# Two-layer causal attention on one Trainium2 core: the next unit's mask put between two divisions, query norms put ahead of the next input, first and last slots laid out anew

## What is computed

```python
x = x + L0(x)          # x: (64, 128, 512) float32
x = x + L1(x)

def L0(x):
    xn = layernorm(x) * g_in
    q  = (xn @ Wq) * 64 ** -0.5          # 16 heads of 64
    k, v = split(xn @ Wkv)               # one key/value head, shared by all
    k, v = null row put in front of each
    sim = q k^T + bias                   # bias: (16, 128, 128), and a null column
    sim = -max above the diagonal and at masked keys
    return layernorm(softmax(sim) v @ Wo) * g_out

def L1(x):                               # as L0, but
    q = q / |q| * q_scale                # each head's query to unit length
    k = k / |k| * k_scale
    bias = a small network of the distance between positions
```

## Time and profile before

| what | value |
|---|---|
| median of 3 runs | 2713.48 us (2711.86 to 2715.43) |
| the profiled execution: its own time | 2714.91 us |
| its span, first to last instruction | 2713.1 us |
| mean granted TensorE clock | 0.984 |
| PE busy | 2523.7 us, 93% |
| VectorE busy | 1849.5 us, 68% |
| ScalarE busy | 1696.9 us, 63% |
| GpSimd busy | 1023.0 us, 38% |
| queries of the late slot awaited by PE, in all | 90.5 us, 64 times |

### The profile page before, as it was taken

The page is one execution under the profiler, slowest core; times in us unless marked ns, Lnnn a source line. Parts: engine busy times, 40 slices in busy tenths (PEclk is TensorE's granted clock), DMA queues, the critical chain, the costliest instruction groups (busy, mean ns, idle before and its releaser), DMA issues.

```text
span 2713.1 us, 47936 instructions
## 1 busy us (share of the span) xinstructions
PE 2523.7 (93%) x13985; PEld 2093.7 (77%) x13985; DVE 1849.5 (68%) x4665; ACT 1696.9 (63%) x6621; POOL 1023.0 (38%) x1688
## 2 busy tenths in 40 slices
PE   2699999999999999999999999999999999999997
PEld 1577877877878888888788788787787787787884
DVE  5467677667667667667667667767767766766764
ACT  2366666666666666666666666666666666666663
POOL 1343343333433433433433334334334333343331
PEclk7799999999999999999999999999999999999998
DMA  6000010010010010000011011001001001001000
GB/s 204 17 30 28 22 33 29 21 33 29 21 33 29 21 33 29 21 33 29 21 33 33 21 29 33 25 25 33 29 21 33 29 21 33 29 21 33 29 17 20
DMA packets 79317, 85.10 MB, mean 31 GB/s; under 512 B 38944, under 2 KB 42048, under 8 KB 79296
## 3 DMA queue, kind: packets, MB, share of 16 engines
q1 hardware_dynamic: 74864, 82.72, 10.0%
q10 hardware_dynamic: 4432, 2.14, 0.4%
HBM read 49.15 MB, written 16.79 MB: 24 GB/s over the span
## 4 chain that ended last, share of the span: by engine, by line
PE 70%; DVE 14%; ACT 10%; issue 3%; DVEq 0%; POOL 0%
PE psum L368 22%; PE psum L300 15%; PE psum L330 13%; PE psum L354 9%; ACT probs L449 7%; PE psum L317 5%; PE psum L339 3%; DVE q_sb L529 3%; DVE xn L490 2%; DVE norm_sq L515 2%; PE psum L287 2%; DVE bn_in L483 2%; DVE probs L546 1%; DVE neg_max L552 1%; DVE k_dup L527 1%
## 5 line engine op out<-in xcount | busy, mean ns | idle before, releaser
L633 POOL TENSOR_TENSOR weights<-probs,den_inv 128x256 f32<-128x256 f32 (+1 forms) x1024 | 492.6, 507 | 1598.8 <-DVE den_inv L558 1598.8
L449 ACT ACTIVATE probs<-probs,neg_max 128x129 f32<-128x129 f32 (+1 forms) x2048 | 744.1, 366 | 507.4 <-DVE neg_max L552 507.4
L622 POOL TENSOR_TENSOR masked_bias<-bias,pad_neg 128x516 f32<-128x516 f32 (+1 forms) x512 | 477.8, 965 | 15.3 <-POOL pad_neg L616 9.2
L546 DVE TENSOR_TENSOR probs<-psum,masked_bias 128x388 f32<-128x388 f32 x512 | 287.3, 562 | 266.7 <-PE psum L330 247.1
L330 PEld LDWEIGHTS psum<-keys,q_t 128*128 128x128 f32 x2048 | 297.4, 188 | 130.7 <-issue 101.9
L330 PE MATMUL psum<-keys,q_t 128*128 128x130 f32 (+1 forms) x2048 | 392.3, 333 | 2.0 <-DVE keys L538 1.1
L449 ACT ACTIVATION_READ_ACCUMULATOR probs<-probs,neg_max 128x1 f32 x2048 | 387.1, 189 | 0.0
L300 PE MATMUL psum<-w_hi,x_hi 128*128 128x384 f32 x1536 | 348.2, 349 | 3.6 <-DVE x_lo L495 3.6
L300 PE MATMUL psum<-w_hi,x_lo 128*128 128x384 f32 x1536 | 329.7, 337 | 0.0
L300 PE MATMUL psum<-w_lo,x_hi 128*128 128x384 f32 x1536 | 329.5, 337 | 0.0
L368 PE MATMUL psum<-wo_hi,o_hi 128*128 128x512 f32 x1024 | 287.5, 423 | 2.3 <-ACT o_hi L460 2.3
(11 more groups left out here) (108 smaller groups left out, 3306.7 us busy)
## 6 DMA issues: line engine op xcount, KB each, us to landing
xa<-in_x_dram SPq DMA_DIRECT2D x64, 256.0 KB, 2.9
x_res<-in_x_dram SPq DMA_DIRECT2D x64, 256.0 KB, 2.6
x_res<-x SPq DMA_DIRECT2D x64, 256.0 KB, 2.3
out_dram<-x_out SPq DMA_DIRECT2D x64, 256.0 KB, 2.1
raw<-in_L_cond_Wq_dram SPq DMA_DIRECT2D x8, 512.0 KB, 7.6
raw<-in_L_cond_Wo_dram SPq DMA_DIRECT2D x8, 256.0 KB, 3.4
raw<-in_L_cond_Wout_dram SPq DMA_DIRECT2D x8, 256.0 KB, 3.7
v_pair<-v_diff SPq DMA_DIRECT2D x128, 16.0 KB, 1.7
```

What stands on the lines that cost most here:

```text
L449: x_ = nc.scalar.activation(s, s, ACT.Exp, bias=neg_max[:, g, b, e:e + 1], accum_out=den[:, g, b, e:e + 1])
L546: nc.vector.tensor_tensor(probs[:, g, :], SP[g % 2][:, 0:ROW], masked_bias[u.layer][:, g, :], ALU.add).then_inc(biased[g], 1)
L622: m = nc.gpsimd.tensor_tensor(block(masked_bias[u.layer][:, gs, :], b), block(bias[u.layer][:, gs, :], b), pad_neg[u.layer][:, 0:WIDTH[b]] ...
L633: m = nc.gpsimd.tensor_tensor(w, block(probs[:, g, :], b)[:, :, 1:1 + n], den_inv[:, g, b, :].unsqueeze(2).to_broadcast([P, 2, n]), ALU.mult)
```

## The change

It has four parts.

1. `body` is split into `early` and `late` slots, and `run_units` takes these and a third form, `meet`. Within the loop TensorE's order and the order of all engines in the early slot stay as they were, but for GpSimd.
2. GpSimd, in every slot: divisions of groups 0 and 1 of u, mask of w, divisions of groups 2 and 3 of u.
3. Late slot, VectorE: `norms` of banks 0 and 1 and both `unit_q` follow one another; `input_statistics` of the next input comes behind them, `normalise` behind `take_kt`. ScalarE: `square` of bank 1 stands ahead of `inverse_root` of bank 0, and `rstd_of_input` behind the copies of the transposed weights.
4. The first and last slots: A(1) is projected beside the attention of A(0), and the first and last B meet the A before them in a `meet` slot, where v's output product is finished early and B's input is made in the same slot. Ahead of the loop stand five slots (A(0) alone, then the attentions of A(0), A(1), B(0), A(2)), behind it five. The two buffers `v_diff` and `v_pair` go by the unit's number (`side`) in place of its layer, and SP's residual load of A is issued a unit ahead.

```diff
-def run_units(eng, body, nb):
+def run_units(eng, begin, early, late, meet, nb):
     A = lambda a: static_unit(0, a, nb)
     B = lambda b: static_unit(1, b, nb)
-    body(None, None, A(0), None, None)
-    body(A(0), None, A(1), None, None)
-    body(A(1), A(0), A(2), None, B(0))
-    body(A(2), A(1), A(3), B(0), B(1))
+    begin(A(0))
+    early(None, None, A(0), A(1))
+    early(A(0), None, A(1), None)
+    meet(A(1), A(0), B(0), A(2))
+    early(B(0), A(1), A(2), B(1))
+    late(A(2), B(0), B(1), A(3))
     with eng.Fori(3, nb - 1) as i:
...
-        body(a, a_prev, a_next, b_old, b_new)
-    body(A(nb - 1), A(nb - 2), None, B(nb - 3), B(nb - 2))
-    body(None, A(nb - 1), None, B(nb - 2), B(nb - 1))
-    body(None, None, None, B(nb - 1), None)
+        early(b_old, a_prev, a, b_new)
+        late(a, b_old, b_new, a_next)
+    early(B(nb - 3), A(nb - 2), A(nb - 1), B(nb - 2))
+    late(A(nb - 1), B(nb - 3), B(nb - 2), None)
+    meet(B(nb - 2), A(nb - 1), B(nb - 1), None)
+    late(B(nb - 1), B(nb - 2), None, None)
+    late(None, B(nb - 1), None, None)
```

SyncE, TensorE's `meet`, ScalarE, VectorE and GpSimd:

```diff
+            def load_next(u):
+                if u.layer == 0 and not last(u):
+                    wait_apart(sp, xn_done, u.done, sp_passed)
+                    load_xa(u.batch + 1)
+                if not last(u):
+                    wait_apart(sp, pad_neg_done, u.done, sp_passed)
+                    load_keep(u.layer, u.batch + 1)
...
+            def slot(u, v, w, n):
+                run_stages((load_next, w), (copy_v, w), (finish, v))
...
+            def meet(u, v, w, n):
+                run_stages((part(scores, (0, 1)), u), (part(project_out, 0), v), (part(project_out, 1), v),
+                           (part(project_out, 2), v), (part(scores, (2, 3)), u), (transpose_x, w),
+                           (part(project, (2, 0, 1)), w), (part(transpose_p, (0, 1, 2, 3)), u))
+                closing(u, w)
...
+            def unit_queries(u, w):
+                run_stages((part(inverse_root, 2), w), (part(square, 0), w), (part(square, 1), w), (part(inverse_root, 0), w),
+                           (part(take_pt, (0, 1)), u), (part(inverse_root, 1), w), (part(take_pt, (2, 3)), u))
+
+            def late(u, v, w, n):
+                run_stages((part(exponential, (0,)), u), (split_x, w), (part(exponential, (1, 2)), u),
+                           (part(square, 2), w), (part(exponential, (3,)), u))
+                unit_queries(u, w)
+                run_stages((rstd_of_input, n), (take_qt, w), (rstd_of_output, v), (split_o, u))
...
+            def unit_queries(w):
+                run_stages((part(norms, 0), w), (part(norms, 1), w), (part(unit_q, 0), w), (part(unit_q, 1), w))
+
+            def late(u, v, w, n):
+                opening(u, v, w)
+                run_stages((take_kv, w), (part(norms, 2), w), (part(inverse_sum, (2,)), u), (part(unit_q, 2), w),
+                           (part(inverse_sum, (3,)), u))
+                unit_queries(w)
+                run_stages((input_statistics, n), (start_finish, v), (take_kt, w), (normalise, n), (end_finish, v))
+
+            def meet(u, v, w, n):
+                run_stages((part(add_bias, (0, 1)), u), (part(row_max, (0, 1)), u), (split_o, v), (part(inverse_sum, (0, 1)), u),
+                           (start_finish, v), (part(add_bias, (2, 3)), u), (end_finish, v), (input_statistics, w),
+                           (part(row_max, (2, 3)), u), (normalise, w), (part(inverse_sum, (2, 3)), u), (split_x, w),
+                           (take_kv, w), (part(norms, 2), w), (part(unit_q, 2), w))
+                unit_queries(w)
+                run_stages((take_kt, w), (input_statistics, n), (normalise, n))
...
-            def divide(u):
-                for g in range(NG):
+            def divide(u, groups):
+                for g in groups:
...
-            def body(a, a_prev, a_next, b_old, b_new):
-                run_stages((mask_bias, a), (divide, b_old), (mask_bias, b_new), (divide, a))
+            def slot(u, v, w, n):
+                run_stages((part(divide, (0, 1)), u), (mask_bias, w), (part(divide, (2, 3)), u))
```

More of the change, by code:

```diff
@@ L251, in copy_v @@
                 wait_apart(sp, v_ready, u.done, sp_passed)
-                sp.dma_start(v_pair[u.layer][DH:P, 1, :], v_diff[u.layer][0:DH, :]).then_inc(v_pair_loaded[u.layer], 16)
-            def body(a, a_prev, a_next, b_old, b_new):
[L255 to L271, removed]
+                sp.dma_start(v_pair[u.side][DH:P, 1, :], v_diff[u.side][0:DH, :]).then_inc(v_pair_loaded[u.side], 16)
@@ new lines, in last, with finish @@
+            def last(u):
+                return isinstance(u.batch, int) and u.batch == NB - 1
+            def load_next(u):
[5 more added lines that the diff above has]
+                    load_keep(u.layer, u.batch + 1)
+            def finish(u):
+                wait_apart(sp, layer_done[u.layer], u.sdone, sp_passed)
+                if u.layer == 0:
+                    if not last(u):
+                        load_x_res(u.batch + 1)
+                else:
+                    sp.dma_start(out[u.batch], x_out[:, :]).then_inc(out_stored, 16)
+                if (u.layer == 1 and not last(u)) or (u.layer == 0 and isinstance(u.batch, int) and u.batch == 0):
@@ L461, in split_o @@
                                          bias=null_v_col[:, 0:1]).then_inc(o_hi_done[b], 1)
[L463 to L472, removed]
@@ L476, in _ @@
+            run_units(act, rstd_of_input, early, late, meet, NB)
         @program.vector
@@ L590, in opening, with begin @@
                            (part(inverse_sum, (0, 1)), u), (part(add_bias, (2, 3)), u), (part(row_max, (2, 3)), u))
[L592 to L600, removed]
+            def begin(u):
+                run_stages((input_statistics, u), (normalise, u))
@@ new lines, in early, with late @@
+            def early(u, v, w, n):
+                opening(u, v, w)
+                run_stages((start_finish, v), (part(inverse_sum, (2,)), u), (take_kv, w), (end_finish, v),
+                           (part(inverse_sum, (3,)), u), (input_statistics, n), (normalise, n), (take_kt, w))
+            def unit_queries(w):
+                run_stages((part(norms, 0), w), (part(norms, 1), w), (part(unit_q, 0), w), (part(unit_q, 1), w))
+            def late(u, v, w, n):
+                opening(u, v, w)
+                run_stages((take_kv, w), (part(norms, 2), w), (part(inverse_sum, (2,)), u), (part(unit_q, 2), w),
+                           (part(inverse_sum, (3,)), u))
+                unit_queries(w)
+                run_stages((input_statistics, n), (start_finish, v), (take_kt, w), (normalise, n), (end_finish, v))
@@ L604, in _ @@
             dve.wait_ge(v_pair_zeroed, 2)
-            run_units(dve, body, NB)
+            run_units(dve, begin, early, late, meet, NB)
         @program.gpsimd
```

62 lines of the change are left out of this document (34 added, 28 removed).

## The result

The changed kernel takes 2617.26 us (median of 4 runs, 2616.14 to 2618.22) against 2713.74 us (4 runs) before: a ratio of 0.9644, interval 0.9628 to 0.9661. The forecast was 2617. Its profiled execution has a span of 2615.0 us, 98.1 us less than before.

The account below looks back on a forecast made before the run. PE, busy 93%, was taken as the bound, its query wait as the largest loss. Gains of 85.8 (loop), 1, 5 and 4.5 us, 96.3 off 2714.9, then 1.4 for the median, gave 2617 us; range 2601 to 2640.

Parts of the forecast that it names:

- The mask's place: GpSimd, late slot: mask between divisions runs 1342.7 to 1346.85; division 2 starts 0.4 us later, costing PE nothing.
- Five columns: VectorE, late slot: bank 2's floor, now beside the mask, taken as held, about 0.7 us; bank 0's root 0.13 us later.
- Query chain: Late slot, square to scaled queries: L529 of bank 1 starts at 1350.74 instead of 1352.58; the 1.58 us excess wait vanishes.
- Keys: Late slot: keys ready at 1354.68, wanted by scores at 1354.55; a 0.15 us wait per turn replaces the old one.
- First and last slots: Outside the loop: 5 us gained at the start, 4.5 us at the end, with `meet` slots of 32.2 us.
- the small late stalls: The two late slots outside the loop: stalls of about 0.9 and 0.3 us go, 1 us gained.
- Rival 1: Late slot: the query wait moves only in part, keys 0.5 us later; 2647 us at worst, from 2630 on; chance 0.15.
- Rivals 2 and 3: Late slot: keys later, 2729 us (chance 0.03); or query wait becomes equal key wait, 2703 to 2715 us (0.02).
- rival 4: Loop and ends: five columns unheld, clock kept in both `meet` slots and at the end; 16 us more, 2601 us; chance 0.06.

Follow-up runs that it names:

- e1: The changed kernel with GpSimd's order put back (whole mask first, then the four divisions, in every slot): 2661.39 us, ratio 0.9816.
- e2: The changed kernel with the late slot's old order of VectorE and ScalarE put back, the mask left between the divisions: 2637.00 us, ratio 0.9725.
- e6: The changed kernel with ScalarE's square of bank 1 put back behind the root of bank 0: 2645.52 us, ratio 0.9759.
- e5: The changed kernel with the keys written (take_kt) ahead of start_finish on VectorE in the late slot: 2596.81 us, ratio 0.9579.
- e3: The changed kernel with the loop's order of all engines as in the kernel before, first and last slots as changed: 2706.85 us, ratio 0.9985.

## Why the prediction was right, and where it was not

| step | predicted | measured |
|---|---|---|
| L562 of bank 1, from the start of the transposes of weights | 2.43 us | 2.34 us |
| keys written, from the same mark | 6.37 us | 6.32 us |
| scores of w, from the same mark | 6.42 us | 6.46 us |
| wait of PE for keys, per turn | 0.15 us | 0.27 us |
| period of the loop | 38.93 us | 38.97 us |
| loop with the slots between A(3)'s and B(62)'s key transposes | 85.8 us and part of 1 us gained | 82.9 us gained |
| first scores of B(0) | 140.9 us | 140.58 us |
| a `meet` slot, from first scores to first scores | 32.2 us | 31.7 us (108.85 to 140.58) and 31.5 us |
| from B(63)'s first scores to the end | as long as before | 3.3 us shorter |

- *The mask's place.* Right, and e1 and e2 show it from both sides. Nothing on PE waits for divisions 2 and 3 in the loop. Division 2 started behind its own sums ([0.18 <-DVE den_inv L591] in the row above), not behind the mask, so the 0.4 us that the prediction gave it did not arise this way.
- *Five columns.* Taken as held: right. Its size was predicted at about 0.7 us and is 0.50. By the rule of the Trainium skill (VectorE: DVE Perf Modes, "What auto-detection actually checks") five in and five out may use both read ports. The trace agrees in that this floor is held beside GpSimd like the six-column ones, with 497 ns as the mean of 59 over the loop where it was 172 before. But the cost that the prediction hung on it, 0.13 us per turn, is nil: ScalarE's logarithm behind it starts without an idle gap, at the end of the exponentials.
- *Query chain.* Right within 0.1 us. Of its links the square's move is shown alone (e6: 27 us), the others only together.
- *Keys.* The mechanism was right, the size was low by half (0.27 for 0.15 us). Three terms of it were off. The prediction's own numbers give 0.18 us and not 0.15 (1354.68 + 0.05 - 1354.55). The signal from the keys' end to the scores was put at 0.05 us and takes 0.13 in the mean. And PE is ready sooner: the prediction took the early slot's 0.17 us between the key's and the queries' transposes as the distance without a wait; with queries that come early it is 0.11 us. The keys themselves came 0.05 us sooner than reckoned. Since PE's readiness makes the recovered wait larger too, the period is off by 0.04 us only. Against e5, where nothing waits and the scores start 2.94 us behind the key's transpose, the 3.28 us of the changed kernel are 0.34 us too many; removing them takes 21 us off.
- *First and last slots.* The sum predicted, 10.5 us and the small late stalls among them, was low: from the first key transpose to the sixth it took 112.6 us and takes 105.7, from B(62)'s key transpose to the last instruction 70.1 and 61.5, together 15.5 us. By the prediction's own marks the first scores of B(0) come 5.6 us sooner (said: 5), and the last meeting is 4.9 us shorter (said: 4.5, where its numbers give 2682.77 - 2678.5, so 4.3). The mis-sized term is what follows the first scores of B(63): put at nothing in the sum, with 3.4 us named as a bound, it gave 3.3 us, as the values and the first output product of B(63) now run at the fast clock. What the start's gain hangs on was not seen. "The projections of A(1) move beside the attention of A(0)" gains nothing by itself (e3); it needs the mask between the divisions. The prediction had priced that mask's cost there (0.5 us) and not that, with the mask first, four divisions queue behind the wait for A(0)'s biases.
- *Luck in the sum.* From B(0)'s to B(62)'s first scores, the loop and its two late neighbours, 84.3 us are gained where 86.8 were forecast; the ends give 13.8 us in place of 9.5. The two errors go against each other and leave 98.1 us for 96.3. That the median lies within 1 us of the forecast is luck; the parts are 2 to 4 us off.

Rival 1 (a part of the wait stays) did not occur: the floor of bank 1 shows 0.17 us. Rivals 2 and 3 needed L529's successor to stay where it was; it came forward by 1.9 us, counted from the transposes of the weights. Of rival 4 only the clock at the end came; the five columns were held, and in both `meet` slots three to four groups of projections ran at the lower clock.

## What to carry to other kernels

An instruction that looks long in one row may be short and held: compare its duration over places with another engine busy and idle, then move the other engine's work to where nothing of that form runs, which here gave three quarters of the loop's gain without touching the waiting engine (e2). When a wait is removed, lay the new order on the old times until the next signal that the engine waits for; here the keys lay 0.3 us behind, and writing them a step earlier was worth another 21 us (e5). In an in-order queue look for the work whose own wait is longest (the mask behind another unit's biases) and put it behind whatever others wait for.

## What was not expected of the hardware

A VectorE `tensor_scalar` on five columns is held by GpSimd as one on six is (0.17 to 0.50 us, and 0.17 to 1.04 us), while a reciprocal on four columns is not (0.18 us at 1296.56, within the divisions that began at 1295.97). The lower clock after an idle PE takes back part of what is won just ahead of it: 1.6 us less idling gave 0.65 us.
